# Row maxima of the attention scores: of three PSUM banks, two are read by one VectorE instruction over 1024 columns and the third by its own

## What is computed

```python
# 16 sub-heads of width 8, values of width 16 for 8 heads, 2 x 1024 tokens
q = rope(xn @ Wq.T) * scaling;  k = rope(xn @ Wk.T);  v = xn @ Wv.T
scores = einsum('bhtd,bhsd->bhts', q, k)
probs  = softmax(scores)                     # needs the maximum of each row of scores
diff   = probs[:, :, 0] - lam * probs[:, :, 1]
attn   = rmsnorm(einsum('bhts,bhsd->bhtd', diff, v)) * (1 - LAMBDA_INIT)
zone   = sum over the top 3 of 8 zones of  gelu(xn @ Wa[e]) @ Wb[e] * w
out    = x + attn @ Wo.T + xn + zone
```

## Time and profile before

| what | before |
|---|---|
| median of three runs | 549.23 us |
| the profiled execution: time | 547.23 us |
| its span, from the first to the last instruction | 545.4 us |
| TensorE matmul busy | 517.8 us (95%) |
| TensorE weight loads busy (beside the matmuls) | 295.6 us (54%) |
| VectorE busy | 458.2 us (84%), 800 instructions |
| ScalarE busy | 339.3 us (62%) |
| reductions of line 683 | 512 in all, mean 688 ns |
| mean granted clock of TensorE | 0.981 |

### The profile page before, as it was taken

One profiled execution on the slowest core, in us unless ns is written; L12 is line 12 of the kernel. 1 busy time (PEld: TensorE's weight loads), 2 busy tenths in 40 slices (PEclk: granted clock), 3 DMA queues, 4 the chain that ended last, 5 costly groups with the idle time before them and its releaser, 6 DMA issues.

```text
span 545.4 us, 8613 instructions
## 1 busy us (share of the span) xinstructions
PE 517.8 (95%) x2607; PEld 295.6 (54%) x2607; DVE 458.2 (84%) x800; ACT 339.3 (62%) x424; POOL 68.8 (13%) x69
## 2 busy tenths in 40 slices
PE   6586999999999999999999999999999999999995
PEld 5564677777555554545555454555545455554333
DVE  2986778999889999999999999999999999998116
ACT  1440687666757666675766666666666666666872
POOL 3186961300000000000000000000000000000000
PEclk9697999999999999999999999999999999999999
DMA  9135526100000010020002001000200020000002
GB/s 314 53 108 199 176 100 199 55 1 2 0 2 1 13 58 2 1 70 0 1 1 67 1 0 46 23 1 0 69 1 0 2 67 3 0 2 1 2 2 77
DMA packets 11771, 23.46 MB, mean 43 GB/s; under 512 B 1490, under 2 KB 6226, under 8 KB 11618
## 3 DMA queue, kind: packets, MB, share of 16 engines
q1 hardware_dynamic: 11314, 20.34, 11.7%
q10 hardware_dynamic: 432, 2.81, 1.4%
HBM read 14.43 MB, written 8.39 MB: 42 GB/s over the span
## 4 chain that ended last, share of the span: by engine, by line
PE 74%; DVE 14%; DMA 4%; ACT 3%; issue 2%; POOL 1%; SPq 1%; ACTq 0%; DVEq 0%; POOLq 0%
PE ps L994 24%; PE ps L1023 23%; PE ps L1016 22%; DVE part_max L683 4%; DVE hL L722 4%; DMA X<-in_x 2%; ACT h L478 1%; PE ps L937 1%; DVE wbH L628 1%; DMA q_scr<-ropeL 1%; ACT hH L481 1%; DVE wbL L630 1%; DMA wb_raw<-in_wb 1%; PE ps L1010 1%; PE ps L862 1%
## 5 line engine op out<-in xcount | busy, mean ns | idle before, releaser
L683 DVE TENSOR_REDUCE part_max<-ps 128x1 f32<-128x512 f32 x512 | 340.1, 688 | 25.4 <-PE ps L994 22.3
L512 ACT ACTIVATE E<-ps 128x1024 f32<-128x1024 f32 x256 | 248.2, 1022 | 125.0 <-PE ps L1016 125.0
L994 PE MATMUL ps<-K,Q 128*128 128x512 f32 x512 | 193.7, 421 | 0.8 <-DVE part_max L683 0.3
L1016 PE MATMUL ps<-Q,K 128*128 128x512 f32 x512 | 161.4, 399 | 0.2 <-ACT zT L486 0.2
L994 PEld LDWEIGHTS ps<-K,Q 128*128 128x128 f32 x512 | 96.0, 188 | 119.3 <-DVE part_max L683 100.7
L1023 PE MATMUL ps<-E,Vg 128*32 128x512 f32 x1024 | 136.4, 605 | 0.6 <-ACT E L512 0.6
L1016 PEld LDWEIGHTS ps<-Q,K 128*128 128x128 f32 x512 | 94.8, 188 | 27.7 <-ACT E L512 10.3
L417 POOL TENSOR_TENSOR U<-AT,rsum 128x256 f32 (+1 forms) x15 | 9.3, 623 | 392.2 <-DVE rsum L776 392.2
L478 ACT ACTIVATE h<-ps 128x512 f32<-128x512 f32 x48 | 28.6, 595 | 38.0 <-PE ps L864 30.8
L722 DVE TENSOR_TENSOR hL<-h,hH 128x512 fp32r<-128x512 f32 x48 | 37.8, 802 | 8.0 <-ACT hH L481 8.0
L1023 PEld LDWEIGHTS ps<-E,Vg 128*32 128x32 f32 x1024 | 20.1, 108 | 44.7 <-issue 34.9
(11 more groups left out here) (140 smaller groups left out, 321.9 us busy)
## 6 DMA issues: line engine op xcount, KB each, us to landing
Q<-q_scr SPq DMA_DIRECT2D x8, 512.0 KB
K<-k_scr SPq DMA_DIRECT2D x32, 96.0 KB
tab<-in_tables ACTq DMA_DIRECT2D x1, 2048.0 KB, 11.4
q_scr<-ropeL SPq DMA_DIRECT2D x4, 512.0 KB, 5.7
q_scr<-ropeH SPq DMA_DIRECT2D x4, 512.0 KB, 4.6
k_scr<-ropeH SPq DMA_DIRECT2D x4, 512.0 KB, 5.1
wa_raw<-in_wa SPq DMA_DIRECT2D x6, 256.0 KB, 3.0
wb_raw<-in_wb SPq DMA_DIRECT2D x6, 256.0 KB, 3.6
```

What stands on the lines that cost most here:

```text
L512: nc.scalar.activation(E[:, par, 2 * jj:2 * jj + 2, :].rearrange("p j t -> p (j t)"), ps[:, 2 * jj:2 * jj + 2, :].rearrange("p j t -> p (j ...
L683: nc.vector.tensor_reduce(part_max[:, half, col, sh:sh + 1], ps[:, ring_bank(x), :], AX.X, ALU.max).then_inc(slot_read, 1)
L994: mm(ps[:, ring_bank(x + sh), :], Q[:, g % 2, k // GJ * P:(k // GJ + 1) * P], K[:, g % 2, k % GJ, sh * BANK:(sh + 1) * BANK], start=True, ...
L1016: last = mm(ps[:, j, :], K[:, par, j, st * P:(st + 1) * P], Q[:, par, th * BANK:(th + 1) * BANK], start=True, stop=True)
```

## The change

`RING` is now (4, 5, 6) and `B_PV` is bank 7. In the steps the slots go round the three banks as before, but slots 3k and 3k+1 (banks 4 and 5) are reduced by one instruction of 128x1024 into two neighbouring columns of `part_max`, after which `slot_read` rises by two; slot 3k+2 (bank 6) is reduced by its own. In the lead both banks of a unit are reduced by one instruction, and TensorE waits before a unit until all earlier slots are read. The half's transpose comes after the unit with remainder 2 of 16 instead of 1, so that its slot is always one in bank 6 (in the lead bank 4 is used for it). The lead has 22 units instead of 24, without turns 4 and 5. `part_max` is filled in the order of the units and line 703 puts the result in order. `HEADS_AT` is (22, 23, 29).

```diff
--- before.py
+++ after.py
@@ -56,8 +56,8 @@
 UG = TB * GJ
 ALL_UNITS = GROUPS * UG
 BEHIND = 4
-LEAD = 24
-LEAD_AT = (4, 5, 6, 7, 8, 9, 10, 11, 12, 13, 14, 15, 16, 17, 18, 20, 21, 22, 24, 25, 26, 28, 29, 30)
+LEAD = 22
+LEAD_AT = (6, 7, 8, 9, 10, 11, 12, 13, 14, 15, 16, 17, 18, 20, 21, 22, 24, 25, 26, 28, 29, 30)
 assert len(LEAD_AT) == LEAD
 
 
@@ -76,17 +76,17 @@
 
 
 
-LEAD_RING, RING, B_PV = (4, 5), (4, 5, 7), 6
+LEAD_RING, RING, B_PV = (4, 5), (4, 5, 6), 7
 assert PAIR_SLOTS % len(RING) == 0
 
 
 def unit_slot(v):
 
-    return 2 * v + max(0, (v - 2) // (UG // 2))
+    return 2 * v + max(0, (v - 3) // (UG // 2))
 
 
 LEAD_SLOTS = unit_slot(LEAD)
-HEADS_AT = (21, 22, 29)
+HEADS_AT = (22, 23, 29)
 TAIL_ORDER = (0, 1, 3, 2)
 HEADS_BANK = RING + (0,)
 O_BANK = (1, 2, 3, B_PV)
@@ -95,7 +95,12 @@
 
 def ring_bank(x):
 
-    return LEAD_RING[x % 2] if x < LEAD_SLOTS else RING[x % 3]
+
+
+    return RING[x % 3]
+
+
+assert LEAD_SLOTS % 3 == 0 and HALF_SLOTS % 3 == 0 and (UG + 6) % 3 == 2
 
 
 def proj_bank(k):
@@ -119,9 +124,14 @@
     return c if rest == 0 and 0 <= c < CHUNKS else None
 
 
+def split_bank(x):
+
+    return LEAD_RING[0] if x < LEAD_SLOTS else ring_bank(x)
+
+
 def half_slot(hx):
 
-    return HALF_SLOTS * hx + UG + 4
+    return HALF_SLOTS * hx + UG + 6
 
 
 
@@ -192,6 +202,7 @@
         ident = cst[:, C_ID:C_ID + P]
         ones = cst[:, C_ONE:C_ONE + P]
         RES = XN
+        parts = part_max[:].rearrange("p h u s -> p (h u s)")
 
         sq = [V1[:, k * BANK:(k + 1) * BANK] for k in range(2)]
 
@@ -678,16 +689,20 @@
             for m in range(6, 8):
                 rotary(m)
 
-            def reduce_bank(slot, x, half, col, sh):
-                dve.wait_ge(slot_made, slot + 1)
-                nc.vector.tensor_reduce(part_max[:, half, col, sh:sh + 1], ps[:, ring_bank(x), :], AX.X,
-                                        ALU.max).then_inc(slot_read, 1)
+            def reduce_pair(end, i):
+                dve.wait_ge(slot_made, end)
+                nc.vector.tensor_reduce(parts[:, i:i + 2], ps[:, RING[0]:RING[0] + 2, :], AX.X,
+                                        ALU.max).then_inc(slot_read, 2)
+
+            def reduce_single(end, i):
+                dve.wait_ge(slot_made, end)
+                nc.vector.tensor_reduce(parts[:, i:i + 1], ps[:, RING[2], :], AX.X, ALU.max).then_inc(slot_read, 1)
 
             def max_split(hx, half, slot, x):
                 dve.wait_ge(slot_made, slot + 1)
-                nc.vector.tensor_copy(maxH[:, half, :], ps[0:16, ring_bank(x), 0:P]).then_inc(maxh_done, 1)
+                nc.vector.tensor_copy(maxH[:, half, :], ps[0:16, split_bank(x), 0:P]).then_inc(maxh_done, 1)
                 dve.wait_ge(maxh_done, hx + 1)
-                nc.vector.tensor_tensor(maxL[:, half, :], ps[0:16, ring_bank(x), 0:P], maxH[:, half, :],
+                nc.vector.tensor_tensor(maxL[:, half, :], ps[0:16, split_bank(x), 0:P], maxH[:, half, :],
                                         ALU.subtract).then_inc(slot_read, 1)
 
             def max_unit(it, o, last):
@@ -696,13 +711,20 @@
                     return
                 x, k, h = unit_slot(o), o % UG, o // (UG // 2)
                 base = PAIR_SLOTS * it
-                for sh in range(2):
-                    reduce_bank(base + x + sh, x + sh, h % 2, k % GJ * FC + k // GJ % FC, sh)
+                if x < LEAD_SLOTS:
+                    reduce_pair(x + 2, 2 * k)
+                else:
+                    for sh in range(2):
+                        if (x + sh) % 3 == 1:
+                            reduce_pair(base + x + sh + 1, 2 * k + sh - 1)
+                        if (x + sh) % 3 == 2:
+                            reduce_single(base + x + sh + 1, 2 * k + sh)
                 if o % (UG // 2) == UG // 2 - 1:
                     dve.wait_ge(slot_read, base + x + 2)
-                    nc.vector.tensor_reduce(neg_max[:, h % 2, :], part_max[:, h % 2, :, :], AX.X, ALU.max,
+                    nc.vector.tensor_reduce(neg_max[:, h % 2, :].rearrange("p (j t) -> p t j", j=GJ),
+                                            part_max[:, h % 2, :, :].rearrange("p (t j) s -> p t j s", j=GJ), AX.X, ALU.max,
                                             negate=True).then_inc(neg_done, 1)
-                if o % (UG // 2) == 1 and h:
+                if o % (UG // 2) == 2 and h:
                     max_split(4 * it + h - 1, (h - 1) % 2, base + half_slot(h - 1), half_slot(h - 1))
                 if last and 2 * PAIR * it + o == ALL_UNITS - 1:
                     max_split(2 * GROUPS - 1, 1, SLOTS - 1, SLOTS - 1)
@@ -977,8 +999,8 @@
 
             def half_transpose(hx, half, slot, x):
                 pe.wait_ge(neg_done, hx + 1)
-                pe.wait_ge(slot_read, slot - (1 if x < LEAD_SLOTS else 2))
-                nc.tensor.transpose(ps[0:16, ring_bank(x), 0:P], neg_max[:, half, :], ident).then_inc(slot_made, 1)
+                pe.wait_ge(slot_read, slot if x < LEAD_SLOTS else slot - 2)
+                nc.tensor.transpose(ps[0:16, split_bank(x), 0:P], neg_max[:, half, :], ident).then_inc(slot_made, 1)
 
             def max_slot(it, o, sh, last):
 
@@ -988,12 +1010,14 @@
                 base = PAIR_SLOTS * it
                 if k == 0 and sh == 0:
                     pe.wait_ge(kq_in, 16 * (GJ + 1) * (2 * it + g + 1))
-                back_to = 1 if x < LEAD_SLOTS else 2
-                if x + sh > back_to:
-                    pe.wait_ge(slot_read, base + x + sh - back_to)
-                mm(ps[:, ring_bank(x + sh), :], Q[:, g % 2, k // GJ * P:(k // GJ + 1) * P],
+                lead = x < LEAD_SLOTS
+                if lead and x and sh == 0:
+                    pe.wait_ge(slot_read, x)
+                if not lead:
+                    pe.wait_ge(slot_read, base + x + sh - 2)
+                mm(ps[:, LEAD_RING[sh] if lead else ring_bank(x + sh), :], Q[:, g % 2, k // GJ * P:(k // GJ + 1) * P],
                    K[:, g % 2, k % GJ, sh * BANK:(sh + 1) * BANK], start=True, stop=True).then_inc(slot_made, 1)
-                if o % (UG // 2) == 1 and h and sh:
+                if o % (UG // 2) == 2 and h and sh:
                     half_transpose(4 * it + h - 1, (h - 1) % 2, base + half_slot(h - 1), half_slot(h - 1))
 
             def heads_sum(c):
```

## The result

| | before | after |
|---|---|---|
| median | 549.33 us (4 runs, 548.25 to 552.34) | 633.83 us (4 runs, 632.80 to 634.63) |
| profiled execution: time, span | 547.23, 545.4 us | 632.80, 631.0 us |
| TensorE busy (share of the span) | 517.8 us (95%) | 545.7 us (86%) |
| VectorE busy, instructions | 458.2 us (84%), 800 | 432.2 us (68%), 617 |
| share of the chain: TensorE, VectorE | 74%, 14% | 53%, 28% |

The ratio is 1.1527, 95% interval 1.1478 to 1.1576: the change makes the kernel 15% slower. 621.2 was forecast.

The account below looks back on a forecast made before the run. TensorE was taken to bound the steps, with VectorE's reads hidden. Stalls 57.3, the rows' DMA 12.3, the lead 1.5 and the tail 0.9 sum to 72.0 us more: profiled 619.2, median 621.2 us, range 596 to 644.

Parts of the forecast that it names:

- A: Step whose first two maxima matmuls are a pair; the fourth waits for that read: 0.87 us, 30 times.
- A with transpose: Same kind of step with the row maxima's transpose in the single's place; the third maxima matmul stalls 0.97 us, 14 times.
- B: Step whose first maxima matmul completes the previous step's pair; its third waits for that read: 0.40 us, 30 times.
- C: Step with single, pair, single; the next step's first maxima matmul waits for the pair: 0.13 us, 43 times.
- m0: First of a step's four maxima matmuls; its load is exposed, its bank ready at 0.53 us.
- the rows' DMA: After the moved transpose, the next step's scores wait for the maxima rows to land: 0.88 us, 14 times, 12.3 us.
- the tail and the rest: After the steps with maxima: one 3.06 us step more, one 2.12 us step without maxima fewer, +0.9 us.
- What bounds the kernel: In the steps TensorE alone bounds; reads are hidden, so VectorE's 28 us saving is worth nothing.
- The price of a wide read: A 1024-column VectorE read takes 1.225 us, from the slope between 32 and 512 columns; a pair saves about 0.15 us.
- The rival that it is hidden: Rows' DMA after the moved transpose is not late, landing faster or scores coming later anyway: 609 us, chance 0.10.
- Ahead of the steps: In the lead, wide-read waits cost 6.8 us against 4.4 now; two units fewer take 0.9 away: net +1.5 us.
- The clock: Rival for the steps: TensorE's clock falls to its lower level in the gaps, 35 us more, 656 us, chance 0.03.

Follow-up runs that it names:

- the kernel with 73 wide reads: Kernel before with ring 4, 5, 6, each step's last two maxima matmuls read as a pair where banks neighbour, except in transpose steps: 549.85 us, ratio 1.0014.
- the last experiment: Kernel before with 22 units in the lead instead of 24, heads one step later, single reads everywhere: 548.30 us, ratio 0.9978.

## Why the prediction was right, and where it was short

The direction and the mechanism held; the sum was 12.6 us too low. Between the profiled executions 85.6 us lie, 72.0 were forecast; that is 13.6 too few, of which 1.0 came back because the median lies 1.0 above the profiled execution and not 2.0. Term by term, from the lengths of the steps:

| term | forecast | measured |
|---|---|---|
| A, 30 times | 0.87, 26.1 us | 0.95, 28.5 us |
| A with transpose, 14 | 0.97, 13.6 | 4.24 - 3.19 = 1.05, 14.7 |
| B, 30 | 0.40, 12.0 | 0.49, 14.7 |
| C (m0 of the next A), 43 | 0.13, 5.6 | 0.22, 9.5 |
| the rows' DMA, 14 | 0.88, 12.3 | 4.24 - 3.28 = 0.96, 13.4 |
| the lead | +1.5 | +4.3 (first step at 148.74 instead of 144.43) |
| the tail and the rest | +0.9 | +0.5, what is left of 85.6 |

- **What bounds the kernel.** Right. Cheaper reads gain nothing in the steps: shown by the kernel with 73 wide reads and an unchanged time. One step of the prediction's reasoning does not follow: it takes VectorE's 0.37 us of idle time in each step for the case of an engine that makes others wait. In the ten steps of the earlier trace rows it made nobody wait; it does so in the changed kernel.
- **The price of a wide read.** 1.225 us, right to the nanosecond. Some luck is in that: the slope came from one read of a PSUM bank and one of 32 columns that lie in `part_max`, and no row showed that the two belong on one line. Its start was not right. I took 0.42 us from the matmul to the read, from the single reads of the earlier trace rows. A read that raises the semaphore by two has an instruction of its own for the wait, and it starts 0.07 to 0.08 later. That failed in every stall at the ring: each is 0.08 to 0.09 above its forecast, 117 times, about 10 us. With the increment of one, A, B and C are within 0.02 of the forecast.
- **The three kinds of step, their counts and stalls.** Right, and the split of cause too: with two single reads in the same places the steps have the same lengths.
- **The transpose that moves.** Right: 13.5 us less without the DMA, 12.3 forecast. The 0.08 that each wait is longer than forecast has another source than the late start of the reads, since it stands with the increment of one too; it is open. The rival that it is hidden falls. Its place costs in two ways, as the kernel with single reads shows; in the changed kernel the stall at the ring hides part of the DMA, which is why 1.2 us there is 0.96 here.
- **Ahead of the steps.** Wrong in size: +4.3 for +1.5. The executions differ before the lead already: the load of the feed-forward part that the last experiment shows comes at 86.9 to 89.7 us in the changed kernel and the five that share its lead. So I count from that load. In the changed kernel it stands at 87.01, the load of the first step at 148.47: 61.46 us. The kernel before takes 57.28 and the one with the shorter lead 56.56. So the two units fewer gave back 0.7 for 0.9, and reading 22 units wide cost 4.9 where 6.8 - 4.4 = 2.4 were forecast. The kernel with the increment of one takes 60.33, so 1.1 of the missing 2.5 is the late start (a loop was forecast at 2.03 us and is 2.11). The 1.5 for the transpose in the lead was right (it waits 1.48). One wait was not in the list. Behind the last wide read, VectorE has the addition of line 736, for which the first scores wait:

```profile
145.62 1.23 DVE L694 TENSOR_REDUCE part_max<-ps 128x2 f32<-128x1024 f32 x1 [0.90 <-PE ps L1018]
...
146.77 0.68 DVE L736 TENSOR_TENSOR XN<-ps,X 128x512 f32<-128x512 f32 x1
...
147.59 0.71 PE L1040 MATMUL ps<-Q,K 128*128 128x512 f32 x2 [0.48 <-DVE XN L736]
```

  That is 0.48 us, but in the kernel before TensorE stands idle for 0.22 at the same place, for ScalarE's `zT`; so it adds at most 0.26. What makes the other 1.1 us is open.
- **The clock.** Its rival falls: the granted clock is 1.00 in the stretch of the steps.
- **Sign and range.** 633.8 lies in 596 to 644, towards the upper end, because nearly all that was missed had one sign: added latencies in closed chains. The upper end itself stood for a dearer wide read, which did not come; that it covered a late start was luck.

Still open is whether a step with wide reads could beat the kernel before. With 10.6 us taken off VectorE nothing was gained, and TensorE is busy throughout; no kernel here tried it with a shorter step of TensorE.

## What to carry to other kernels

A wide read of several banks saves one fixed cost (here 0.15 us) but keeps all its banks from the first write to the end of the read. In a ring, count for each writer how long after the last write of the group it comes; if that is less than latency plus the whole read (here 2.0 us from the load of the group's last matmul to the next load, 299.94 to 301.94), every turn stalls by the difference, whatever the engine's busy share says. Where the reading engine is not the bound, as in these steps, the saving is worth nothing; where it nearly is, as in this lead, a ring of just one group turns two overlapping engines into a closed loop. Count the slots that rare steps (a transpose) take, too: they shift who waits for whom.

## What the runs showed of the hardware

The wide reduction, a VectorE instruction that waits for one semaphore and raises another by two, is preceded by an instruction of its own for the wait (183 of 21 ns; none when it raises it by one), and starts 0.49 us after the start of the matmul that it waits for instead of 0.44. With 183 such reads in closed chains that cost 9.6 us (633.83 against 624.21). The Trainium skill, page "Perfetto Trace Analysis", section "Identifying Dependency Chains", knows such inserted instructions for waits on several engines; here the instruction waits for one.
